# First stage: tiles of octets two to four turned on VectorE and by transfers, instead of on TensorE

## The chip, the cores and the metric

The kernel runs on one core of a Trainium2 chip. The metric is the device time of one execution in microseconds (us), the median of several runs. The core has TensorE (PE in the rows), VectorE (DVE), ScalarE (ACT), GpSimd (POOL) and SyncE (SP), and 16 DMA engines that SyncE and GpSimd issue transfers to.

## The reference

A gated cross-attention layer and a gated mixture-of-experts layer, over x of 32 batches x 64 tokens x 512 and a context of the same shape:

```python
x = x + tanh(g_xattn) * attn(layernorm(x), ctx)
x = x + tanh(g_ffn) * moe(layernorm(x))
# in attn: keys and values from context and latents together
hidden_states = jnp.concatenate([context, latents], axis=1)
q = (latents @ Wq)                       # 32 heads of 128
k = (hidden_states @ Wk)                 # 4 heads of 128
v = (hidden_states @ Wv)
```

The change concerns only the first stage, which makes k and v and the turned, normalised x from which the second stage makes q. Attention, the output projection (second stage) and the experts (third stage) are as they were.

## The kernel before, in words

x and the context are 2048 tokens each. They are worked in four **octets** of 512 tokens (o = 0 to 3; "octet 1" in the text and in the comments below is o = 0, so octets 2 to 4 are the changed ones). An octet has 8 **units**: four 128-token tiles of the context (src 0) and four of the normalised x (src 1). For every unit four 128x128 transposes on TensorE (L414, `transposes`) put the tile, features on partitions, into a PSUM tile `ps_t`; ScalarE copies it rounded into `tok_hi` (L273, `tok`), VectorE writes the remainder into `tok_lo` (L342, `tok_low`). All products are made in three passes of rounded parts (L84 to L86). A **V job** (`v_job`, one per unit, 12 matmuls) makes the values of 128 tokens in `ps_v`, which ScalarE copies out (L282, `v_copy`); a **K job** (`k_job`, 8 per octet, 12 matmuls) makes a head's keys of 512 tokens of one source in `ps_k`, which VectorE copies out (L352, `k_copy`). `ps_v` and `ps_k` have two banks each, so job n waits for the copy of job n - 2. `tok_hi` and `tok_lo` have two buffers, one per octet in turn.

The order on every engine is written out by hand, and every engine works strictly in its own order. TensorE: for an octet its 8 V jobs, each with the next unit's transposes ahead of it, then its 8 K jobs, with the next octet's first transposes before the sixth. VectorE: the low parts and normalisations (L336, `normalise`, into one of two `normed` buffers) between, and in octet 1's K phase the statistics of the last eight x tiles (L316, L319). ScalarE: the high part of the next unit, then the V copy. SyncE issues all loads and stores: the next octet's context tiles (L206, L207) before the last V store, the stores of V (L213), of the turned x (L219) and of K (L237). GpSimd makes constants and loads the two gates (L252), and has nothing more to do in this stage. In the profile the block transpose on VectorE stands only in the second stage (L1013, issued on by L774, read back by L783), and GpSimd's indirect transfers only in the third (L1693, L1703).

Of the kernel before, what the change touches and what calls it, by code (L numbers as in the profile page):

```python
# [27 lines left out]
P = 128  # L28
# [4 lines left out]
C = D // P  # L33
# [59 lines left out]
def stage_one(nc, a, common, scratch):  # L93
# [25 lines left out]
    with ExitStack() as stack:  # L119
# [12 lines left out]
        normed = [b.sb(f"normed{i}", [P, D]) for i in range(2)]  # L132
        stats = b.sb("stats", [P, TILES, 6])
# [10 lines left out]
        x_in = [b.sem(f"x_in{i}") for i in range(OCTETS)]  # L144
        ctx_in = [b.sem(f"ctx_in{i}") for i in range(2)]
        kv_in = [b.sem(f"kv_in{i}") for i in range(4)]
        gates_in = b.sem("gates_in")
# [19 lines left out]
        x_stored = [b.sem(f"x_stored{i}") for i in range(2)]  # L167

# [4 lines left out]
        UNITS = 8  # L173

        def unit(o, u):

            return (u // 4, u % 4) if o == 0 else (u % 2, u // 2)
# [7 lines left out]
        def _(sp):  # L185
# [13 lines left out]

            for o in range(OCTETS):  # L200
                for u in range(UNITS):
                    src, i = unit(o, u)

                    if u == 7 and o + 1 < OCTETS:
                        sp.wait_ge(transposed, UNITS * o + 7)
                        sp.dma_start(ctx_raw[:, 0], ctx_v[o + 1][:, 0]).then_inc(ctx_in[0], 16)  # L206
                        sp.dma_start(ctx_raw[:, 1:4], ctx_v[o + 1][:, 1:4]).then_inc(ctx_in[1], 16)  # L207
# [8 lines left out]
                    if u in (5 if o == 0 else 4, 7):  # L216
# [11 lines left out]
                if o == OCTETS - 1:  # L228
# [24 lines left out]

        @block.scalar
        def _(act):
# [5 lines left out]
            def split_hi(piece, hi):  # L261
                act.wait_ge(kv_in[piece], 16)
# [3 lines left out]
            def tok(o, u):  # L266
                src, i = unit(o, u)

                act.wait_ge(transposed, UNITS * o + u + 1)
                if u == 0 and o >= 2:  # L270

                    act.wait_ge(x_stored[o % 2], 64)
                act.activation(tok_hi[o % 2][:, src, :, i * P:(i + 1) * P], ps_t[u % 2][:],  # L273
                               ACT.Copy).then_inc(tok_hi_made, 1)
# [10 lines left out]
            tok(0, 0)  # L285
            split_hi(0, wv_hi)
            split_hi(1, wv_hi)
            for o in range(OCTETS):
                for u in range(UNITS):
                    if u + 1 < UNITS:  # L290
                        tok(o, u + 1)
# [1940 lines left out]
```

## Time and profile before

| | |
|---|---|
| median of 3 runs | 1464.78 us (1463.96 to 1466.05) |
| the profiled execution: span | 1485.9 us |
| its own time beside the span | not recorded apart; the span stands for it |
| first stage, to the last K job | 200.8 us of the span |
| mean granted TensorE clock | 0.987 |

The rows are those of one profiled execution; their times are microseconds from its start. "Idle before" in brackets is how long the engine had stood still and what ended it. In the rows an instruction's duration runs to its end; the next one of the same engine often starts a little before that, so that the pitch from start to start is what a queue of them takes.

### The profile page before, as it was taken

What the parts mean: (1) busy time and instruction counts of PE and PEld (TensorE: products, weight loads), DVE (VectorE), ACT (ScalarE), POOL (GpSimd) and SP (SyncE); (2) the same over time, 40 slices, a digit from 0 to 9 for tenths busy, and PEclk for the clock granted to TensorE, in tenths of its full rate; (3) what the DMA queues carried; (4) which work ended last, traced back from release to release, by engine and by line L of the source; (5) the groups of instructions that cost most, each with busy time, mean ns of one, the idle gap of its engine ahead of it and who ended that gap; (6) DMA issues with size and microseconds to landing.
All of it is one profiled execution on the core that took longest, in us unless ns stands there. A gap on an engine that the chain in (4) does not pass through costs nothing.

```text
span 1485.9 us, 24374 instructions
## 1 busy us (share of the span) xinstructions
PE 1416.6 (95%) x8624; PEld 1253.0 (84%) x8624; DVE 1041.1 (70%) x1682; ACT 785.9 (53%) x2029; POOL 191.1 (13%) x200
## 2 busy tenths in 40 slices
PE   7999988999999999999999999999998899989885
PEld 6888887999999899999899999899997588888774
DVE  4422238777788777787877787887787587656657
ACT  4212226555566555566655566655555445767660
POOL 0000000000000000000000000000026124777740
PEclk9999999999999999999999999999999999999998
DMA  8576555344454433463443365444324206876419
GB/s 264 156 231 170 142 198 157 123 135 125 149 179 146 139 121 121 161 180 127 142 150 118 123 179 167 133 136 138 119 90 144 99 1 211 258 252 212 150 29 339
DMA packets 189622, 230.98 MB, mean 155 GB/s; under 512 B 22675, under 2 KB 123063, under 8 KB 185418
## 3 DMA queue, kind: packets, MB, share of 16 engines
q1 hardware_dynamic: 179530, 212.77, 45.3%
q0 software_dynamic: 9984, 16.82, 3.5%
q8 instruction: 62, 1.02, 0.3%
q14 instruction: 46, 0.38, 0.1%
HBM read 161.85 MB, written 83.36 MB: 165 GB/s over the span
## 4 chain that ended last, share of the span: by engine, by line
PE 67%; DVE 6%; ACT 5%; issue 3%; DMA 2%; another core or an unknown queue 2%; SPq 0%; ACTq 0%; POOL 0%; DVEq 0%; POOLq 0%
PE ps_q L84 8%; PE ps_y L84 8%; PE ps_y L86 7%; PE ps_y L85 7%; PE ps_q L85 7%; PE ps_q L86 7%; PE ps_s L1082 5%; PE bank L84 3%; PE bank L86 3%; PE bank L85 2%; PE ps_s L1084 2%; PE ps_o L84 2%; PE ps_o L86 2%; PE ps_o L85 2%
## 5 line engine op out<-in xcount | busy, mean ns | idle before, releaser
L84 PE MATMUL ps_q<-xt,wq_hi 128*128 128x256 f32 x1024 | 296.3, 289 | 2.3 <-PEq L119 1.7
L85 PE MATMUL ps_q<-xt,wq_lo 128*128 128x256 f32 x1024 | 289.4, 283 | 0.0
L86 PE MATMUL ps_q<-xt,wq_hi 128*128 128x256 f32 x1024 | 289.4, 283 | 0.0
L903 ACT ACTIVATE s_sb<-s_sb,nmax 128x128 f32<-128x128 f32 x512 | 200.5, 394 | 148.5 <-DVE nmax L991 148.5
L84 PE MATMUL ps_y<-wo_hi,o_hi 128*128 128x512 f32 x512 | 204.6, 400 | 7.2 <-DVE wo_lo L935 3.6
L86 PE MATMUL ps_y<-wo_lo,o_hi 128*128 128x512 f32 x512 | 203.5, 398 | 0.0
L85 PE MATMUL ps_y<-wo_hi,o_lo 128*128 128x512 f32 x512 | 202.6, 396 | 0.0
L84 PEld LDWEIGHTS ps_q<-xt,wq_hi 128*128 128x128 f32 x1024 | 195.2, 191 | 2.9 <-issue 2.1
L85 PEld LDWEIGHTS ps_q<-xt,wq_lo 128*128 128x128 f32 x1024 | 195.8, 191 | 0.0
L86 PEld LDWEIGHTS ps_q<-xt,wq_hi 128*128 128x128 f32 x1024 | 195.6, 191 | 0.0
L883 ACT ACTIVATE o_hi<-ps_o 128x512 fp32r<-128x512 f32 x128 | 76.1, 595 | 183.2 <-PE ps_o L86 183.0
L980 DVE TENSOR_TENSOR o_lo<-ps_o,o_hi 128x512 fp32r<-128x512 f32 x128 | 88.2, 689 | 79.4 <-ACT o_hi L883 79.4
L940 DVE TENSOR_TENSOR q_lo<-ps_q,q_hi 128x512 fp32r<-128x512 f32 x128 | 88.5, 691 | 69.5 <-ACT q_hi L859 69.5
L1082 PE MATMUL ps_s<-kt,q_hi 128*128 128x256 f32 x512 | 125.5, 322 | 3.1 <-DVE q_lo L940 2.1
L84 PEld LDWEIGHTS ps_y<-wo_hi,o_hi 128*128 128x128 f32 x512 | 97.2, 190 | 27.0 <-DVE wo_lo L935 4.2
L556 POOL TENSOR_TENSOR trial<-root 128x9 f32<-128x9 f32 (+1 forms) x6 | 1.7, 284 | 904.3 <-DVE root L578 904.0
L86 PEld LDWEIGHTS ps_y<-wo_lo,o_hi 128*128 128x128 f32 x512 | 97.0, 189 | 23.2
L1084 PE MATMUL ps_s<-kt,q_lo 128*128 128x128 f32 x512 | 114.3, 223 | 0.0
L85 PEld LDWEIGHTS ps_y<-wo_hi,o_lo 128*128 128x128 f32 x512 | 97.3, 190 | 18.4
L1082 PEld LDWEIGHTS ps_s<-kt,q_hi 128*128 128x128 f32 x512 | 96.6, 189 | 10.0 <-issue 2.7
L1084 PEld LDWEIGHTS ps_s<-kt,q_lo 128*128 128x128 f32 x512 | 97.8, 191 | 6.2
L989 DVE TENSOR_TENSOR s_sb<-ps_s,s_cross 128x512 f32<-128x512 f32 x128 | 88.1, 688 | 18.0 <-ACT s_cross L889 17.8
(261 smaller groups left out, 3160.2 us busy)
## 6 DMA issues: line engine op xcount, KB each, us to landing
xt<-x_scratch SPq DMA_DIRECT2D x32, 1024.0 KB, 5.6
p_table<-p_blocks SPq DMA_DIRECT2D x128, 256.0 KB, 2.0
p_lo<-p_table SPq DMA_DIRECT2D x512, 64.0 KB, 2.1
w_raw<-in_L_ffn_ew SPq DMA_DIRECT2D x93, 256.0 KB
v_full<-v_out SPq DMA_DIRECT2D x64, 128.0 KB, 2.6
k_full<-k_out SPq DMA_DIRECT2D x16, 512.0 KB, 2.8
w_raw<-in_L_xattn_Wq SPq DMA_DIRECT2D x16, 512.0 KB, 5.9
kt_raw<-k_full SPq DMA_DIRECT2D x32, 256.0 KB, 2.8
```

What stands on the lines that cost most here:

```text
L84: pe.matmul(out, w_hi, x_hi, start=first, stop=False)
L85: pe.matmul(out, w_lo, x_hi, start=False, stop=False)
L86: return pe.matmul(out, w_hi, x_lo, start=False, stop=last)
L556: then(pool.tensor_tensor(w, r, r, ALU.mult))
L883: act.activation(o_hi[s.last_parity][:, :, s.last_token], ps_o[:], ACT.Copy).then_inc(o_hi_made, 1)
L903: last = act.activation(s_sb[:, i], s_sb[:, i], ACT.Exp, bias=nmax[:, i:i + 1], accum_out=sums[:, i:i + 1])
L940: dve.tensor_tensor(by_heads(q_lo[quad_parity], p), ps_q[p % 2][:].rearrange("p (h b t) -> p h b t", h=2, b=QB), f32(by_heads(q_hi[quad_pa ...
L980: dve.tensor_tensor(o_lo[s.last_parity][:, :, s.last_token], ps_o[:], f32(o_hi[s.last_parity][:, :, s.last_token]), ALU.subtract).then_inc ...
L989: dve.tensor_tensor(s_sb[:], ps_s[:, :, 0], s_cross[:], ALU.add).then_inc(folded, 1)
L1082: pe.matmul(ps_s[:, i], q_hi[quad_parity][:, batch, heads].rearrange("p h t -> p (h t)"), k[:, :, batch], start=True, stop=False)
L1084: last = pe.matmul(ps_s[:, i, 0], q_lo[quad_parity][:, batch, heads].rearrange("p h t -> p (h t)"), k[:, 0, batch], start=False, stop=True)
```

## The change

Octet 1 stays as it was, with transposes on TensorE. For octets 2 to 4 TensorE has no transposes. VectorE turns each tile of 128x512 in 32x32 blocks into `blocks` (`turn`), context tiles from `ctx_raw`, x tiles from `normed`. When the four tiles of one source are turned, GpSimd issues 16 transfers (`move`) that carry block row i, block column j of all of them to partitions 32j to 32j + 31 of `turned`. ScalarE makes `tok_hi` from `turned` (`tok_turned`) and VectorE `tok_lo` (`tok_turned_low`). There is one `blocks` and one `turned`, both of 8 KB a partition. So the turns of x wait until the context's move has landed, and a move waits until the low parts of what stood in `turned` are made. The context of an octet is loaded by four transfers instead of two, in an order of rows that suits the blocks, and earlier. Units of all octets now go context first, then x. The statistics of tiles 8 to 15 move from octet 1's K phase to the start of octet 2's V phase, and their square root on ScalarE behind octet 2's third V copy. x stores come after units 6 and 8. Some semaphores are shared (the last two x loads, the two Wk loads).

```diff
+        blocks = b.sb("blocks", [P, 4, C, 4, 32])
+        turned = b.sb("turned", [P, C, 4, 4, 32])
...
+        ctx_rows = a["ctx_4096"].rearrange("b s d -> (b s) d").rearrange("(o i t s) d -> o t i s d", i=4, t=4, s=32)
+        def unit(u):
+            return u // 4, u % 4
+        def blocks_by(o, src):
+            return UNITS * (o - 1) + 4 * src + 4
+        def moves_by(o, src):
+            return 256 * (2 * (o - 1) + src + 1)
...
+            def load_ctx(o):
+                for t in range(4):
+                    sp.dma_start(ctx_raw[:, t], ctx_rows[o, t]).then_inc(ctx_in[1], 16)
...
+                    if o == 0 and u == 4:
+                        sp.wait_ge(transposed, 4)
+                        load_ctx(1)
+                    if 0 < o < OCTETS - 1 and u == 2:
+                        if o + 2 < OCTETS:
+                            sp.wait_ge(blocks_made, blocks_by(o + 1, 0))
+                            load_ctx(o + 2)
...
+                if o == 0:
+                    sp.wait_ge(blocks_made, blocks_by(1, 0))
+                    load_ctx(2)
...
+            def move(o, src):
+                pool.wait_ge(blocks_made, blocks_by(o, src))
+                if src or o > 1:
+                    pool.wait_ge(tok_lo_made, UNITS * o + 4 * src)
+                for i in range(4):
+                    for j in range(4):
+                        pool.dma_start(turned[32 * j:32 * j + 32, :, i].rearrange("p c t s -> p c (t s)"),
+                                     blocks[32 * i:32 * i + 32, j].rearrange("p c t s -> p c (t s)")
+                                     ).then_inc(moved, 16)
...
+            def tok_turned(o, u):
+                src, i = unit(u)
                 if u == 0 and o >= 2:
 
                     act.wait_ge(x_stored[o % 2], 64)
+                act.wait_ge(moved, moves_by(o, src))
+                act.activation(tok_part(tok_hi[o % 2], u), turned_part(u), ACT.Copy).then_inc(tok_hi_made, 1)
...
+                    if o == 1 and u == 2:
+                        std_of(8, TILES)
+                    if 0 < o < OCTETS - 1 and u in (3, 4):
+                        tok_turned(o + 1, 2 * u - 6)
+                        tok_turned(o + 1, 2 * u - 5)
                 if o == 0:
                     std_of(4, 8)
+                    for u in range(4):
+                        tok_turned(1, u)
                 if o + 1 < OCTETS:
-                    tok(o + 1, 0)
+                    for u in range(4, UNITS):
+                        tok_turned(o + 1, u)
...
+            def turn(o, u):
+                src, t = unit(u)
+                if t == 0 and (src or o > 1):
+                    dve.wait_ge(moved, moves_by(o, src) - 256)
+                if src:
+                    dve.wait_ge(normed_made, 4 * o + t + 1)
+                else:
+                    dve.wait_ge(ctx_in[1], 16 + 64 * o)
+                tile = normed[t % 2][:] if src else ctx_raw[:, t, :]
+                dve.transpose(blocks[:, :, :, t, :], tile.rearrange("p (c j r) -> p j c r", c=C, j=4)
+                              ).then_inc(blocks_made, 1)
...
+            turn_ctx(1)
+            for job in range(UNITS):
+                k_copy(0, job)
+                if job == 1:
+                    turn_x(1)
+                if job in (2, 3):
+                    tok_turned_low(1, 2 * job - 4)
+                    tok_turned_low(1, 2 * job - 3)
+                if job in (6, 7):
+                    tok_turned_low(1, 2 * job - 8)
+                    tok_turned_low(1, 2 * job - 7)
+            for o in range(1, OCTETS):
+                if o + 1 < OCTETS:
+                    turn_ctx(o + 1)
+                    if o == 1:
+                        dve.wait_ge(late_in, 32)
+                        stats_of(8, TILES)
+                        rstd_of(8, TILES, 3)
+                    turn_x(o + 1)
+                    for u in range(4):
+                        tok_turned_low(o + 1, u)
                 for job in range(UNITS):
                     k_copy(o, job)
+                    if o + 1 < OCTETS and job < 4:
+                        tok_turned_low(o + 1, 4 + job)
```

On VectorE, from the reciprocal of octet 1's second normalisation through the K copies of octet 1, the order before was:

```order
L323 RECIPROCAL rstd<-std 128x4
L352 COPY k_out<-ps_k 128x8x64
L336 TENSOR_SCALAR normed<-y,mean_var,rstd 128x512
L352 COPY k_out<-ps_k 128x8x64
L336 TENSOR_SCALAR normed<-y,mean_var,rstd 128x512
L352 COPY k_out<-ps_k 128x8x64
L316 BN_STATS stats<-y 128x6 x2
L319 BN_AGGR mean_var<-stats 128x2 x2
L352 COPY k_out<-ps_k 128x8x64
```

and is now:

```order
L378 RECIPROCAL rstd<-std 128x4
L411 STREAM_TRANSPOSE blocks<-ctx_raw 128x16x32 x4
L425 COPY k_out<-ps_k 128x8x64 x2
L392 TENSOR_SCALAR normed<-y,mean_var,rstd 128x512 x2
L411 STREAM_TRANSPOSE blocks<-normed 128x16x32
L392 TENSOR_SCALAR normed<-y,mean_var,rstd 128x512
L411 STREAM_TRANSPOSE blocks<-normed 128x16x32
L392 TENSOR_SCALAR normed<-y,mean_var,rstd 128x512
L411 STREAM_TRANSPOSE blocks<-normed 128x16x32 x2
L425 COPY k_out<-ps_k 128x8x64
L416 TENSOR_TENSOR tok_lo<-turned,tok_hi 128x4x128 x2
L425 COPY k_out<-ps_k 128x8x64
```

The third K copy now stands behind the first turn of a normalised tile, which waits for the move of the context tiles.

On ScalarE, from the end of octet 1's V phase into octet 2's, the order is now (`turned` is the tile that the moves fill, `std` the square root for the normalisation):

```order
L302 ACTIVATE std<-mean_var,eps 128x4
L322 ACTIVATE tok_hi<-turned 128x4x128 x8
L359 ACTIVATE ones_r<-ones 128x128
L361 ACT_TABLE_LOAD
L361 ACTIVATE gain_attn<-gates 128x1
L362 ACTIVATE gain_ffn<-gates 128x1
L330 ACTIVATE v_out<-ps_v 128x512 x3
L302 ACT_TABLE_LOAD
L302 ACTIVATE std<-mean_var,eps 128x8
L330 ACTIVATE v_out<-ps_v 128x512
L322 ACTIVATE tok_hi<-turned 128x4x128 x2
L330 ACTIVATE v_out<-ps_v 128x512
```

All eight high parts of octet 2 stand ahead of its first V copy, and the next octet's between the fourth, fifth and later ones; before, each high part stood just ahead of the V copy of the unit before it.

## Rows read from the trace of the kernel before

**Rows 1.** The page: busy us, share of the span, instructions
```profile
PE 1416.6 (95%) x8624; PEld 1253.0 (84%) x8624; DVE 1041.1 (70%) x1682; ACT 785.9 (53%) x2029; POOL 191.1 (13%) x200
```

**Rows 2.** By stretch: length, busy us of PE, PEld, DVE, ACT, POOL, clock, DMA share
```profile
36.60:58.90 22.30, 22.30 (x102) 18.41 (x101) 12.25 (x28) 3.46 (x8) 0.00 (x0) 1.00 0.63 206
...
84.20:106.30 22.10, 22.10 (x101) 18.21 (x101) 6.44 (x10) 1.20 (x2) 0.00 (x0) 1.00 0.87 280
...
179.00:200.80 21.80, 21.77 (x97) 17.68 (x95) 4.84 (x7) 0.60 (x1) 0.00 (x0) 1.00 0.43 138
```

**Rows 3.** Timeline of ScalarE, V copies: start, us, what, idle before
```profile
24.16 0.60 ACT L282 ACTIVATE v_out<-ps_v 128x512 f32<-128x512 f32 x1 [2.17 <-PE ps_v L86]
...
62.26 0.60 ACT L282 ACTIVATE v_out<-ps_v 128x512 f32<-128x512 f32 x1 [2.17 <-PE ps_v L86]
...
65.47 0.60 ACT L282 ACTIVATE v_out<-ps_v 128x512 f32<-128x512 f32 x1 [2.12 <-PE ps_v L86]
```

**Rows 4.** Timeline of VectorE, first stage
```profile
37.62 0.18 DVE L323 RECIPROCAL rstd<-std 128x4 f32<-128x4 f32 x1 [1.54 <-ACT std L259]
...
89.66 0.69 DVE L352 COPY k_out<-ps_k 128x512 f32<-128x512 f32 x1 [1.57 <-PE ps_k L86]
90.27 0.54 DVE L336 TENSOR_SCALAR normed<-y,mean_var,rstd 128x512 f32<-128x512 f32 x1
92.38 0.69 DVE L352 COPY k_out<-ps_k 128x512 f32<-128x512 f32 x1 [1.57 <-PE ps_k L86]
```

**Rows 5.** Timeline of VectorE, a block transpose of the second stage and its successor
```profile
222.94 0.71 DVE L1013 STREAM_TRANSPOSE p_blocks<-s_sb 128x512 f32<-128x512 f32 x1
223.57 1.18 DVE L935 TENSOR_TENSOR wo_lo<-w_raw,wo_hi 128x1024 fp32r<-128x1024 f32 x1
```

**Rows 6.** Timeline of GpSimd: its plain gate loads, and indirect ones of stage three
```profile
1.96 0.73 POOL L252 DMA_DIRECT2D gates<-in_g_xattn  x1 [0.25 <-issue]
2.69 0.58 POOL L252 DMA_DIRECT2D gates<-in_g_ffn  x1
...
1263.44 1.03 POOL L1703 DMA_INDIRECT slots_y<-y_out,slot_row  x1 [3.16 <-ACT y_out L1811]
1264.78 1.00 POOL L1703 DMA_INDIRECT slots_y<-y_out,slot_row  x1 [0.31 <-issue]
1266.09 1.46 POOL L1693 DMA_INDIRECT rows_in<-xn_table,slot_token  x1 [0.30 <-issue]
```

**Rows 7.** DMA issues: tile, queue, count, KB each, median us to landing
```profile
p_lo<-p_table SPq DMA_DIRECT2D x512, 64.0 KB, 2.1
...
gates<-in_g_xattn POOLq DMA_DIRECT2D x1, 0.5 KB, 6.6
```

**Rows 8.** The line of SyncE's 32-partition transfers: issue ns min/median/max
```profile
L783 SPq DMA_DIRECT2D p_lo<-p_table x512: 302/432/1939, 225.7 to 1159.3; - x171
```

**Rows 9.** Timeline of ScalarE ahead of octet 2
```profile
55.95 0.29 ACT L304 ACTIVATE ones_r<-ones 128x128 fp32r<-128x128 f32 x1
56.26 1.28 ACT L306 ACT_TABLE_LOAD   x1
...
57.66 0.19 ACT L307 ACTIVATE gain_ffn<-gates 128x1 f32<-128x1 f32 x1
```

**Rows 10.** Groups by line, first 209 us: busy us, mean ns, idle before
```profile
L316 DVE BATCH_NORM_STATS2 stats<-y 128x6 f32<-128x512 f32 x16 | 10.3, 679 | 0.0
...
L319 DVE BATCH_NORM_AGGREGATE mean_var<-stats 128x2 f32<-128x6 f32 x16 | 2.3, 170 | 0.1
```

**Rows 11.** Timeline of TensorE: the first and the seventh matmul after its first idle
```profile
7.92 0.77 PE L84 MATMUL ps_v<-wv_hi,tok_hi 128*128 128x512 f32 x1 [3.00 <-DVE wv_lo L328]
...
10.62 0.46 PE L84 MATMUL ps_v<-wv_hi,tok_hi 128*128 128x512 f32 x1
```

**Rows 12.** DMA of the first 209 us: total, and context loads as in rows 7
```profile
DMA packets 38065, 39.36 MB, mean 188 GB/s; under 512 B 1949, under 2 KB 28573, under 8 KB 37906
...
ctx_raw<-in_ctx SPq DMA_DIRECT2D x4, 768.0 KB, 6.4
```

More of the change, by code:

```diff
@@ L142, in stage_one @@
         ps_k = [b.ps(f"ps_k{i}", [P, 512]) for i in range(2)]
-        x_in = [b.sem(f"x_in{i}") for i in range(OCTETS)]
+        gates_in = b.sem("gates_in")
+        late_in = b.sem("late_x_in")
+        x_in = [b.sem(f"x_in{i}") for i in range(2)] + [late_in] * (OCTETS - 2)
         ctx_in = [b.sem(f"ctx_in{i}") for i in range(2)]
-        kv_in = [b.sem(f"kv_in{i}") for i in range(4)]
-        gates_in = b.sem("gates_in")
+        kv_in = [b.sem(f"wv_in{i}") for i in range(2)] + [b.sem("wk_in")] * 2
         consts_made = b.sem("consts_made")
@@ L167, in stage_one @@
         x_stored = [b.sem(f"x_stored{i}") for i in range(2)]
+        blocks_made = b.sem("blocks_made")
+        moved = b.sem("moved")
         x_v = a["x"].rearrange("b s d -> (b s) d").rearrange("(o i p) d -> o p i d", i=4, p=P)
@@ L252, in _ @@
                 pool.dma_start(gates[:, i:i + 1], src).then_inc(gates_in, 16)
+            def move(o, src):
[8 more added lines that the diff above has]
+            for o in range(1, OCTETS):
+                move(o, 0)
+                move(o, 1)
         @block.scalar
@@ L289, in _ @@
                 for u in range(UNITS):
-                    if u + 1 < UNITS:
-                        tok(o, u + 1)
+                    if o == 0 and u + 1 < UNITS:
+                        tok(u + 1)
                     if o == 0 and u == 2:
@@ L353, in k_copy, with turn_ctx, turn_x @@
                                 ps_k[job % 2][:].rearrange("p (q b t) -> p q b t", q=2, b=QB)).then_inc(k_copied, 1)
-            tok_low(0, 0)
+            def turn_ctx(o):
+                for u in range(4):
+                    turn(o, u)
+            def turn_x(o):
+                normalise(4 * o)
+                normalise(4 * o + 1)
+                for t in range(4):
+                    turn(o, 4 + t)
+                    if t < 2:
+                        normalise(4 * o + 2 + t)
+            tok_low(0)
@@ new lines, in _ @@
+            rstd_of(4, 8, 2)
+            turn_ctx(1)
[9 more added lines that the diff above has]
+                    tok_turned_low(1, 2 * job - 7)
+            for o in range(1, OCTETS):
+                if o + 1 < OCTETS:
[5 more added lines that the diff above has]
+                    turn_x(o + 1)
+                    for u in range(4):
+                        tok_turned_low(o + 1, u)
@@ L417, in v_job @@
             def v_job(o, u):
-                src, i = unit(o, u)
+                src, i = unit(u)
                 n = UNITS * o + u
@@ L442, in k_job @@
                 last.then_inc(k_done, 1)
-            transposes(0, 0)
+            transposes(0)
             for o in range(OCTETS):
                 for u in range(UNITS):
-                    if u + 1 < UNITS and not (o == 0 and u == 0):
-                        transposes(o, u + 1)
+                    if o == 0 and 0 < u < UNITS - 1:
+                        transposes(u + 1)
                     v_job(o, u)
                     if o == 0 and u == 0:
-                        transposes(0, 1)
+                        transposes(1)
                 if o == 0:
@@ L454, in _ @@
                 for job in range(UNITS):
-                    if o + 1 < OCTETS and job == 5:
-                        transposes(o + 1, 0)
                     k_job(o, job)
```

114 lines of the change are left out of this document (52 added, 62 removed).

## The prediction

> **What bounds the kernel now.** I read the page first, then the busy time by stretch, then the timelines of the first stage. The page gives TensorE 95% of the span [rows 1]. The change touches the first stage alone, so the question is what sets the pace there. The table by stretch answers it: from 36.6 us, where the K jobs of octet 1 begin, TensorE is busy without a break, at a granted clock of 1.00 (the upper of its two levels, 2.4 GHz), until the stage's last K job is done at 200.8 us; of seven stretches three are shown, and only the last lacks 0.03 us [rows 2]. Every microsecond of TensorE work taken out there is a microsecond won, as long as its operands still come in time. In the rows of VectorE and ScalarE both wait for TensorE: VectorE copied a K result every 2.72 us and stood idle 1.57 us before each copy [rows 4].
>
> **What is removed.** A job of twelve 128x512 matmuls takes 2.72 us alone: K copies start at 89.66 and 92.38 [rows 4]. A V job has the same twelve and one tile's four transposes, and takes 3.21 us: V copies start at 62.26 and 65.47 [rows 3]. A tile's transposes so cost 0.49 us of TensorE. Octets 2 to 4 have 24 tiles: 24 x 0.49 = **11.8 us** less TensorE work. The copies out of PSUM (tok_hi on ScalarE, tok_lo on VectorE) stay in number and only read `turned` instead.
>
> **What is added, and its unit price.** VectorE gets 24 block transposes. The same form and size stands in the second stage at 0.71 us, and the next instruction starts 0.63 us after it [rows 5]. I take 0.63 us a tile; a copy takes 0.61 by the same measure (89.66 to 90.27), and a normalisation, 0.54 long, 0.45 [rows 4].
>
> GpSimd gets 96 transfers in six moves of 16, each with 32 partitions of 4 runs of 512 bytes, 64 KB. No row shows a plain transfer of this size issued by GpSimd. The nearest are its two plain gate loads, 128 pieces each as these have, at 728 and 577 ns back to back [rows 6]. I take the second, since the first also bears the start: 0.58 us. Bounds: below, SyncE issues 32-partition transfers of 64 KB in 0.30 us at least and 0.43 in the median [rows 8]; above, GpSimd's indirect ones start 1.3 us apart [rows 6]. From issue to landing SyncE's 64 KB transfers take 2.1 us in the median [rows 7]; a gate load of GpSimd took 6.6 us amid the first loads [rows 7]. I take 2.1, for its size and its place after the first loads, and keep 6.6 as the end. A **move** so takes 16 x 0.58 + 2.1 = **11.4 us**.
>
> **Where that lies.** `blocks` and `turned` exist once. So VectorE may not turn the normalised tiles before the move of the context tiles has landed, GpSimd may not start the second move before those turns and four tok_lo are done, and in VectorE's and ScalarE's queues copies that TensorE needs stand behind these waits. I walk through it, with TensorE free-running at 2.72 us a job from 36.6 us.
> (a) VectorE finishes the reciprocal at 37.8 [rows 4], turns four context tiles (2.5) by 40.3; move 1 lands at 51.7. Behind the wait VectorE has four turns and two normalisations (3.4) and then the third K copy (0.7): 55.8. TensorE's fifth K job needs that copy and could have started at 36.6 + 4 x 2.72 = 47.5. **Idle 8.3.**
> (b) After the turns (55.1) come two copies and four tok_lo (6 x 0.61): move 2 starts at 58.8, lands at 70.2. ScalarE stands before it; then four tok_hi (0.5 each), the constant, table load and tanh (1.8, [rows 9]) and the first V copy (0.6): 74.6. TensorE did its K jobs by 66.7, two V jobs by 72.1, and needs that copy for the third. **Idle 2.5.**
> (c) VectorE, after tok_hi, has four tok_lo and a K copy (3.0), four turns (2.5): 76.4. Then eight statistics with aggregates, 0.77 each by their starts (0.68 and 0.17 long, [rows 10]) = 6.2; ScalarE waits for them with table load and root (1.5) and the fourth V copy (0.6): 84.7, against TensorE at 74.6 + 3 x 2.72 = 82.8. **Idle 2.0.**
> (d) Move 3 runs from 76.4 to 87.8; ScalarE takes two tok_hi, then the V copy: 89.4, against 87.4. **Idle 2.0.**
> (e) Turns to 91.2, four tok_lo to 93.7, move 4 lands at 105.1; tok_hi, tok_lo and the second K copy: 107.0. TensorE's fourth K job could start at 89.4 + 5 x 2.72 = 103.0. **Idle 4.0.**
> (f) In octet 3 the V copy after move 5 comes just in time (136.8 against 136.9), the K copy behind move 6 does not: 154.6 against 150.5. **Idle 4.0.**
> Octet 4 has no moves. Sum 22.8 of new idle, less 11.8 = **+11.0 us**; each 0.1 us on a move adds some 0.6.
>
> **The rest.** After its first idle TensorE took 2.7 us for six V matmuls, from 7.92 to 10.62 [rows 11], where six at a twelfth of 2.72 take 1.4: 1.3 us lost. I add it once, for the 8.3 us gap; the bounds are 0 and 1.3 for each of (a), (e) and (f). SyncE's context loads become four per octet. The first four go out after octet 1's fourth V copy (24.8, [rows 3]) and its two stores; with 6.4 us to landing [rows 12] they are in by about 35, and the turns start at 37.8: no cost. If that cover went, (a) would start later by the lateness. SyncE gets waits on the turns of the next octet, behind which V stores stand; each is over before the V copy that comes next. The second stage's first transfers wait for stores of octet 4, unchanged. 6 MB more between SBUF and SBUF stand beside 39 MB [rows 12] in a stage whose DMA share is 0.43 to 0.87 [rows 2]; that lies inside 2.1 to 6.6. So 11.0 + 1.3 = **+12.3 us** on the profiled 1485.9, which itself lies 21 us over the median of the runs; I carry the difference to the median: 1464.8 + 12.3 = **1477.1**.
>
> **Rivals.**
> (These times leave the 1.3 out.) *Issues are cheap (the other side).* If GpSimd issued almost as SyncE does at its best (0.30), say 0.34 us, a move is 7.5 us. Then idle is 4.5 in (a), 0.6 in (c) and none elsewhere: 5.1 - 11.8 = -6.7, **1458.1**. It decides at a move of 9.5 us, an issue of 0.46. For it: 32 partitions are fewer than 128. Against: both plain rows are above 0.46. The Trainium skill, "DMA: Bandwidth & Descriptors", section on the anatomy of one DMA on the GpSimd path, calls descriptor generation small and gives about 2.0 us plus bytes over 436 GB/s, which for 1 MB is an estimated 4.4 us a move and some 10 us gained; no plain transfer of size in this trace tests it.
> *Issues are dear.* At the indirect pitch of 1.3 a move is 22.9 us; idle by the same walk is 19.9, 14.0, 2.0, 13.5, 15.6, 11.4 (octet 3 then misses the V copy too) and 15.6: 92.0 - 11.8 = +80, **1545**; at 0.9 it is +42, 1507; at 0.58 but 6.6 to landing, +38, 1503. For it: 4 runs a partition. Against: indirect ones also read indices.
> *VectorE holds GpSimd off.* Most of VectorE's work during the moves reads PSUM, but in (d) the eight statistics run beside move 3. If they kept GpSimd from issuing, move 3 would land 6.2 us later and nothing absorbs it: +18, **1483**. In the trace GpSimd's indirect issues vary only from 1.00 to 1.46 us in a stretch where VectorE works too [rows 6], which speaks for little of it. The Trainium skill, "SBUF — State Buffer", warns that VectorE instructions which take two SBUF ports lock GpSimd's descriptor writing out and puts one DMA at 620 ns alone and about 3100 ns beside such a copy; at that price the change would be far slower, and no row here shows it.
> That the change doesn't do what it says is excluded: TensorE's program lists no transposes after octet 1.
>
> **How the numbers follow.** Forecast (issue 0.50 to 0.75, GpSimd not held off): 0.38, own range 1468 to 1492. Held off: 0.05. Dear: 0.22. Cheap enough to win (under 0.45): 0.27. Near the balance, within 0.2% (2.9 us, what a measurement of this kernel can tell from no change): 0.08. Faster 0.27, same 0.08, slower 0.65. The range goes from 1456 to 1506: it leaves out the upper half of the dear case (0.11) and moves shorter than about 6.5 us (0.05).
>
> **What would show it.** Right: new groups of 96 GpSimd transfers of some 0.58 us, first 16 spanning 9 us from about 40; TensorE idle some 8 us before its fifth K job, waiting for a K copy, and the stage's end near 212 us instead of 200.8. Wrong: GpSimd transfers under 0.45 us and a stage end under 200. The table by stretch says which.

## The result and the profile after

The changed kernel takes **1505.2 us** (median of 4 runs, 1500.4 to 1508.5) beside 1464.7 for the kernel before on the same chip. The ratio is 1.0269, with a 95% interval of 1.0241 to 1.0296, so it is 40.5 us slower. The prediction was 1477.1 us: the sign is right, the loss is more than three times the 12.3 us forecast. Its own range for the forecast (1468 to 1492) missed; the outer range (1456 to 1506) held the time only just.

The busy times of the page after, beside [rows 1]:

```profile
PE 1410.7 (94%) x8528; PEld 1246.9 (83%) x8528; DVE 1053.1 (70%) x1706; ACT 788.3 (52%) x2031; POOL 244.1 (16%) x296
```

TensorE has 96 instructions less (24 tiles of four transposes), GpSimd 96 more, VectorE 24 more. The rest is in where the stage ends. The first matmul of stage two, before and then after, on TensorE's timeline (start, length, idle before it):

```profile
202.51 0.36 PE L84 MATMUL ps_q<-xt,wq_hi 128*128 128x256 f32 x1 [1.74 <-PEq L119]
```
```profile
241.94 0.36 PE L84 MATMUL ps_q<-xt,wq_hi 128*128 128x256 f32 x1 [1.72 <-PEq L119]
```

That is 39.4 us later, nearly all of the 40.5: the loss lies in stage one. (The spans, 1505.9 and 1485.9, are not to be set side by side: behind this start the profiled execution of the kernel before took 1283 us, that of the changed kernel 1264, and those of the thirteen profiled runs below, with the same later stages, 1257 to 1268.) The first stage by stretch, with the columns of [rows 2] (length, busy us of PE, PEld, DVE, ACT, POOL, clock, DMA share, GB/s):

```profile
39.60:61.90 22.30, 11.35 (x49) 8.74 (x47) 4.87 (x9) 0.78 (x2) 8.67 (x16) 0.88 0.83 230
61.90:83.50 21.60, 17.23 (x68) 14.11 (x69) 11.82 (x20) 5.38 (x10) 8.65 (x16) 0.81 0.46 129
83.50:110.00 26.50, 19.54 (x76) 15.33 (x75) 15.60 (x34) 8.18 (x16) 11.05 (x21) 0.87 0.72 184
...
131.00:153.00 22.00, 22.00 (x98) 18.21 (x97) 6.05 (x10) 2.39 (x4) 8.81 (x16) 1.00 0.52 143
153.00:190.00 37.00, 28.63 (x106) 22.61 (x105) 11.78 (x19) 7.49 (x13) 8.64 (x16) 0.82 0.59 152
```

Before, TensorE was busy in every microsecond of such a table and its clock stood at 1.00. Now it stands still for up to half of a stretch, and the granted clock falls in the same stretches. The waits of TensorE from 36 to 242 us say for whom (waited for: us in total, times, longest):

```profile
PE ps_k L84 <- DVE k_out L425: 26.6, 4, 13.2
PE ps_v L84 <- ACT v_out L330: 9.2, 3, 6.7
```

These are copies of K and V results, which stand in VectorE's and ScalarE's queues behind waits for the moves. The moves on GpSimd's timeline (start, length of 16 issues, idle before):

```profile
46.96 8.67 POOL L289 DMA_DIRECT2D turned<-blocks  x16 [43.67 <-DVE blocks L411]
69.81 8.65 POOL L289 DMA_DIRECT2D turned<-blocks  x16 [14.17 <-DVE tok_lo L416]
86.76 8.64 POOL L289 DMA_DIRECT2D turned<-blocks  x16 [8.30 <-DVE blocks L411]
107.59 8.65 POOL L289 DMA_DIRECT2D turned<-blocks  x16 [12.19 <-DVE tok_lo L416]
143.23 8.81 POOL L289 DMA_DIRECT2D turned<-blocks  x16 [26.98 <-DVE blocks L411]
163.24 8.64 POOL L289 DMA_DIRECT2D turned<-blocks  x16 [11.20 <-DVE tok_lo L416]
```

The first instruction that a move releases gives its landing. Two of the six, on VectorE's and ScalarE's timelines:

```profile
61.93 0.71 DVE L411 STREAM_TRANSPOSE blocks<-normed 128x512 f32<-128x512 f32 x1 [13.06 <-DMA turned<-blocks]
```
```profile
177.96 2.19 ACT L322 ACTIVATE tok_hi<-turned 128x512 fp32r<-128x512 f32 x4 [11.61 <-DMA turned<-blocks]
```

The other four land at 80.30, 100.92, 122.06 and 156.56. From first issue to last landing the six take 15.0, 10.5, 14.2, 14.5, 13.3 and 14.7 us, 13.7 in the mean; the forecast had 11.4. I call the part behind the last issue the tail: 6.3, 1.8, 5.5, 5.8, 4.5 and 6.1 us, 5.0 in the mean, where 2.1 was taken.

### The profile page after: what moved, and what is told of

Its sections match the earlier page's. It is cut to its first block, busy times and chain, and to the rows that moved or that the text cites. A ratio compares the mean times of both kernels' runs of the same rounds, so it can differ in the third digit from the quotient of the medians.

```text
span 1505.9 us, 24296 instructions
## 1 busy us (share of the span) xinstructions
PE 1410.7 (94%) x8528; PEld 1246.9 (83%) x8528; DVE 1053.1 (70%) x1706; ACT 788.3 (52%) x2031; POOL 244.1 (16%) x296
## 4 chain that ended last, share of the span: by engine, by line
PE 63%; DVE 7%; issue 4%; DMA 4%; ACT 3%; POOL 3%; ACTq 0%; POOLq 0%; SPq 0%; DVEq 0%
PE ps_q L84 8%; PE ps_y L84 7%; PE ps_y L86 7%; PE ps_y L85 7%; PE ps_q L86 7%; PE ps_q L85 7%; PE ps_s L1173 5%; PE ps_s L1175 2%; PE ps_o L84 2%; PE ps_o L86 2%; PE ps_o L85 2%; PE bank L84 2%; DMA slots_y<-y_out,slot_row 2%; POOL rows_in L1784 2%; DMA w_raw<-in_L_xattn_Wo 2%
## 5 line engine op out<-in xcount | busy, mean ns | idle before, releaser
L84 PEld LDWEIGHTS ps_q<-xt,wq_hi 128*128 128x128 f32 x1024 | 194.8, 190 | 4.1 <-issue 2.1
```

The source lines that it names most:

```text
L84: pe.matmul(out, w_hi, x_hi, start=first, stop=False)
```

## Experiments

Each time stands beside the kernel before in the same set of runs (1463.9, 1465.7, 1465.2, 1464.6 and 1464.5 us in the five sets). Theory A: what costs is the length of the moves, as waits at a few places, with a lower clock behind each stop. Against it stand, in turn, the moves' own bytes, a price of the transfers beyond the waits, and other causes of slow matmuls.

**The changed kernel again.**

> The changed kernel once more, for a second profile of the same program. Theory A (the moves' landing is late because the 16 DMA engines also carry SyncE's loads and stores): issue again 0.54 us each, moves of 10.5 to 15 us with the shortest where the fewest other transfers run, stage one ends at 241 +- 4 us. Theory B (octet 1's 3.0 us and the late context load were chance of one execution): this profile has its first K job near 36.6 us and context tiles turned from 41 us; otherwise near 39.6 and 44 us again.

1504.25 us. Moves of 15.0, 10.6, 13.7, 15.0, 12.3 and 14.7 us; TensorE's stops 2.2, 13.2, 0.2, 6.2, 5.4, 1.2 and 7.7 us. The pattern is the kernel's, not one run's. Octet one again ended late (first K job at 39.5, turns from 44.1), which Theory B of the expectation would not have; the other runs below take it up again.

**No moves at all.** Constant data in `turned`; VectorE's turns stay.

```
-            for o in range(1, OCTETS):
-                move(o, 0)
-                move(o, 1)
+            pool.memset(turned[:]..., 0.5).then_inc(moved, 1)
...
-                act.wait_ge(moved, moves_by(o, src))
+                act.wait_ge(moved, 1)
```

> Leaves out the 96 transfers and the waits for them; turned is filled once with a constant, so keys, values and x of octets 2 to 4 are wrong. Everything else of the change stays (turns on VectorE, copies out of turned, context loads in four, the new orders). Theory A (only the moves cost): the 11.8 us of transposes are won, less up to 3 for octet 1: ratio 0.992 to 0.994 (1453 to 1456 us), stage one ends at 189 to 192 us. Rival R (VectorE's added turns or the new orders on ScalarE cost by themselves): ratio at or over 0.997, and TensorE waits for a copy by VectorE or ScalarE somewhere.

1457.8 us, ratio 0.9960 (0.9946 to 0.9974): 6 us under the kernel before, and between the two expectations (at most 0.994, at least 0.997). Stage two starts at 194.8, 7.7 us earlier than before. The whole loss of the change therefore needs the moves. Of the 4.1 us missing to the 11.8 of removed transposes, 1.3 are a later start of the K jobs (37.9 against 36.6) and 2.2 are one stop, whose cause VectorE's timeline shows:

```profile
42.54 2.49 DVE L407 STREAM_TRANSPOSE blocks<-ctx_raw 128x512 f32<-128x512 f32 x4 [3.44 <-DMA ctx_raw<-in_ctx]
```

Even without moves VectorE waits 3.4 us for octet two's context, which the prediction had in the tile by 35 us; TensorE stops 2.2 us behind it. The row also gives the price of a turn: 2.49 us for four, 0.62 each (taken: 0.63).

**Less store traffic.** V and x stores carry a quarter of their bytes; the rest is written at the stage's end, and that filling is in the time.

```
-   sp.dma_start(dst.rearrange("g t d -> t g d"),
-                v_out[u % 4][64 * bb:64 * bb + 64])
+   sp.dma_start(dst.rearrange("g t d -> t g d")[:, 0:1],
+                v_out[u % 4][64 * bb:64 * bb + 64, 0:1])
```

> The stores of V and of the turned x carry a quarter of their bytes during the stage; the rest of those tensors is filled with other data by extra stores at the stage's end (and two before the first load of x), so results are wrong and the total has that fill in it; only the moves' times in stage one are to be read. Theory A (shared DMA engines): the landing after the last issue of moves 3 to 6, which was 5.5, 5.8, 4.5 and 6.1 us, falls to 2 to 3.5 us. Rival P (32-partition transfers are slow among themselves, or GpSimd's queue lands late by itself): it stays at 4.5 to 6 us.

1537.7 us in all, with the filling, so only the moves are read. Their tails are 5.1, 2.0, 6.2, 6.9, 2.8 and 1.4 us. In moves five and six, beside which mainly the stores run, they fell from 4.5 and 6.1 to 2.8 and 1.4. Moves one, three and four run beside context loads, K stores or the loads for stage two, which were left, and their tails did not fall. The issues took 0.54 us as ever. The expectation had moves three and four fall too; they rose, by 0.6 and 1.1 us. Beside move four this run is no clean test: two of the stores that fill up x, 384 KB each, go out at 109.7 and 110.7, in the middle of it. So moves five and six show that the tail follows the traffic beside the move; for the others this run leaves it open, and the total says nothing here.

**A quarter of the moves' own bytes**, with the same 96 issues.

```
-  pool.dma_start(turned[32*j:32*j+32, :, i]..., blocks[32*i:32*i+32, j]...)
+  pool.dma_start(turned[32*j:32*j+32, 0:1, i]..., blocks[32*i:32*i+32, j, 0:1]...)
```

> The changed kernel, but each of GpSimd's 96 transfers moves one quarter of its columns (32 x 512 bytes instead of 32 x 2048); the rest of turned holds a constant written once, so that the product is not the reference's. The issues stay sixteen a move. Theory A (what a transfer waits for is the other traffic on the shared DMA engines): a move keeps most of its tail beside other traffic, the last transfer landing 3 to 5 us after the last issue in moves 1, 3 and 4, and the time is within 12 us of the changed kernel's 1505. Theory B (the transfers' own bytes make the tail): the tails fall to about 2 us everywhere, moves take 10.7 us, and the time falls by some 20 us to 1485.

1488.0 us in one run, 17 below the changed kernel, between the two expectations (over 1493, and 1485). The tails are 4.3, 1.4, 4.4, 4.7, 1.4 and 3.6 us, 3.3 in the mean instead of 5.0: a quarter of the bytes takes a third of the tail away, and what stays is again long in moves one, three and four. An issue took 496 instead of 548 ns. So both the traffic beside a move and its own bytes count; the time fell with the length of a move, 11.1 us instead of 13.7. What fewer issues, in place of smaller ones, would give was not measured.

**Waits of a set length, without a transfer.** Six, or eight, fills of the same tile on GpSimd take the place of each move.

```
-                        pool.dma_start(turned[32 * j:32 * j + 32, :, i]...
+                for i in range(6):
+                    if done + i:
+                        pool.wait_ge(moved, done + i)
+                    pool.memset(turned[:]..., 0.5).then_inc(moved, 1)
```

> The changed kernel with every move replaced by six fills of the same tile on GpSimd, one behind the other (one took 1.82 us, so some 11 us, the length of a move that the prediction took), with the same waits before and after and no transfer; the product is not the reference's. It shows what moves of the predicted length cost when nothing else about them is left. If the walk of the prediction is right in its terms, 1476 us. Theory A (the excess came from the length of the moves beside other traffic, from a clock that falls after each stop of TensorE, and from late context loads): the clock and the late loads are still there, so 1482 to 1492 us, with matmuls 0.43 us apart behind each stop over 2.3 us. If the time is 1500 or more, the length of the moves is not what matters.

> As the run with six fills, with eight of them (some 14.6 us, about the mean length of the moves as measured). Theory A: 1500 to 1508 us, the changed kernel's time without a single transfer of its own, so that a microsecond on each move costs 5 to 7 us in all. Rival (the transfers cost beyond the wait, by taking DMA time from the loads and stores): under 1495 us.

Six fills: 1486.9 us (ratio 1.0147, 1.0122 to 1.0171). Eight: 1514.7 (1.0332, 1.0315 to 1.0350), above the range that I gave, since the fills took longer than I reckoned. Two of the "moves" of each on GpSimd's timeline, six fills first:

```profile
43.83 11.45 POOL L291 MEMSET turned<- 128x2048 f32 x6 [40.55 <-DVE blocks L411]
62.71 11.16 POOL L291 MEMSET turned<- 128x2048 f32 x6 [7.43 <-DVE tok_lo L416]
```
```profile
44.48 15.18 POOL L291 MEMSET turned<- 128x2048 f32 x8 [41.20 <-DVE blocks L411]
67.08 14.90 POOL L291 MEMSET turned<- 128x2048 f32 x8 [7.43 <-DVE tok_lo L416]
```

The means over six are 11.3 and 15.05 us. So 3.74 us on each move cost 27.8 us, 7.4 us for each (6 to 9 by the intervals of the two ratios). On the line through these two points the changed kernel's 13.7 us give 1504.6; it takes 1505.2 with all its transfers. The run with a quarter of the bytes, at 11.1 us, should take 1485.7 and takes 1488.0. **The time follows from the length of the moves**; in this order of the work no price of the transfers beyond the wait can be seen. The agreement is closer than these runs can tell: the four of one kernel lie 3 to 8 us apart, the changed kernel began its K jobs 2.8 and 2.3 us later than the two runs with fills, and eight fills had stops of 39.9 us in all beside its 35.9. A price of a few us would not show. At the 11.4 us of the forecast the line gives 1487.5, not 1477.1. So of the 28 us missed some 17 are length, and some 10.5 would have been missed at the right length too.

**Context loaded earlier.**

```
-                    if o == 0 and u == 4:
+                    if o == 0 and u == 3:
                         sp.wait_ge(transposed, 4)
                         load_ctx(1)
```

> The changed kernel with one step moved: the loads of the second octet's context stand ahead of the fourth V store in SyncE's queue, not ahead of the fifth; nothing else. The prediction had these loads in by 35 us at no cost. Theory A (VectorE's turns, the moves behind them and the first stop of TensorE wait for these loads, 3.4 us of it): the first move starts some 3 us earlier, at about 43.5, and the time falls by 2 to 6 us. If the loads cost nothing, the time stays within 1 us of 1505.

1501.4 us, 3.8 less, ratio 1.0254 (1.0232 to 1.0276). That is the size expected, but the interval overlaps the changed kernel's, so a gain is likely and not shown. In its profile VectorE no longer waits for the context (0.04 us instead of 3.4), TensorE's early stop of 2.1 us is gone, and the first move starts at 41.9 instead of 47.0, of which 2.2 us come from an octet one that was done earlier in that run. The stop before octet two's fourth K job was longer in return, 7.2 us instead of 5.2.

**Matmuls that nobody reads, in the stops.**

```
+                    if u == 6:
+                        keep_busy(o, (0, 28, 8, 0)[o])
                     v_job(o, u)
...
+                    if job == (4 if o == 0 else 3):
+                        keep_busy(o, (56, 22, 24, 0)[o])
                     k_job(o, job)
```

> The changed kernel with matmuls that nobody reads (into a bank that is free by then) put where TensorE stops: 56 ahead of the fifth K job of the first octet, 28 and 8 ahead of the seventh V jobs of octets two and three, 22 and 24 ahead of their fourth K jobs. At 0.23 us each they are a little shorter than the stops as measured (13.2, 6.7, 2.3, 5.2, 6.1 us). Theory A (after each stop the clock stays at half for some 4 us, about 11 us in all): the matmuls behind the places of the stops stand 0.23 us apart, the granted clock is 0.99 or more from 60 to 200 us, and the time falls by 6 to 11 us, to 1494 to 1499. Rival (the slow matmuls have another cause, the SBUF or the transfers): they stay 0.43 apart and the time stays, or rises by what the added matmuls take.

TensorE's timeline behind the long stop, first in the changed kernel, then with the filling:

```profile
66.27 0.79 PE L84 MATMUL ps_k<-tok_hi,wk_hi 128*128 128x512 f32 x1 [13.23 <-DVE k_out L425]
66.86 0.63 PE L85 MATMUL ps_k<-tok_hi,wk_lo 128*128 128x512 f32 x1
67.29 0.63 PE L86 MATMUL ps_k<-tok_lo,wk_hi 128*128 128x512 f32 x1
...
70.16 0.40 PE L84 MATMUL ps_k<-tok_hi,wk_hi 128*128 128x512 f32 x1
70.39 0.40 PE L85 MATMUL ps_k<-tok_hi,wk_lo 128*128 128x512 f32 x1
```
```profile
64.23 0.39 PE L84 MATMUL ps_k<-tok_hi,wk_hi 128*128 128x512 f32 x1
64.45 0.39 PE L85 MATMUL ps_k<-tok_hi,wk_lo 128*128 128x512 f32 x1
64.68 0.39 PE L86 MATMUL ps_k<-tok_lo,wk_hi 128*128 128x512 f32 x1
```

With TensorE kept busy the matmuls stand 0.23 us apart at once; idle before them, they stood 0.43 apart for 3.9 us. The granted clock over the two stretches (the column behind POOL's, in shares of 2.4 GHz) is 0.50, which is 1.2 GHz, and 1.00:

```profile
66.30:70.00 3.70, 3.70 (x9) 2.92 (x10) 2.92 (x5) 0.00 (x0) 0.20 (x1) 0.50 0.46 171
```
```profile
64.20:68.00 3.80, 3.80 (x18) 3.15 (x17) 3.13 (x6) 0.00 (x0) 0.78 (x2) 1.00 0.52 194
```

So it is the clock, and the rival falls. Over the stage I count 50 matmuls about 0.43 apart after the change, 10.5 us more than at 0.23, and 15 with the filling, 3.0 us. But the time is 1501.6 us, 3.6 less where I expected 6 to 11, and not surely less (1.0249, 1.0227 to 1.0270, which overlaps the changed kernel's). TensorE still waits 8.7 us beside the filling:

```profile
PE ps_k L84 <- DVE k_out L425: 7.0, 3, 3.1
PE ps_v L84 <- ACT v_out L330: 1.7, 2, 1.2
```

At these places the chain of moves sets the pace. A faster TensorE only comes earlier to the next wait. So the 7.5 us of slow matmuls that went gave back some 3.6; by the two intervals it can be anything from nothing to all of it. That they are worth less than their length is likely, from the waits that remain, and not shown.

**Another order of the work.** In octets two to four TensorE runs the four V and the four K jobs of the context, then those of x; the other engines wait for a move only where its tiles are next. The first context load stands one V store earlier, as in the run above.

```
+                    if o and u == 3:
+                        for job in range(4):
+                            k_job(o, job)
...
-                g, src = job // 2, job % 2
+                g, src = (job % 4, job // 4) if o else (job // 2, job % 2)
```

> The changed kernel in another order: in octets two to four TensorE runs the four V jobs of the context, the four K jobs of the context, the four V jobs of x, the four K jobs of x; ACT and VectorE wait for a move only where its tiles are next, and the first context load is issued one V store earlier. The moves and their transfers are the same. Theory A (the cost is the wait at a few places, not the transfers themselves): each move now has some 20 us of cover, the stops of TensorE shrink to under 4 us in sum, and the time is 1457 to 1466 us. Rival (GpSimd's transfers slow the whole stage, by VectorE or by the DMA engines): 1480 us or more.

1474.3 us (1.0065, 1.0047 to 1.0083): 31 less than the changed kernel with the same 96 transfers, so the rival, at 1480 or more, is out. It also missed my 1457 to 1466. The largest stop left, 5.1 us, has a new cause, on VectorE:

```profile
129.27 0.69 DVE L423 COPY k_out<-ps_k 128x512 f32<-128x512 f32 x1 [15.12 <-DMA k_full<-k_out]
130.88 0.69 DVE L423 COPY k_out<-ps_k 128x512 f32<-128x512 f32 x1 [0.92 <-DMA k_full<-k_out]
```

A K result can't be copied before the K store of the octet before has left its tile; in this order that copy comes sooner, and the store went out late.

**The same with that mended**: K stores ahead of the loads for stage two, low parts of x ahead of the fourth K copy.

```
                 if o == 1:
+                    store_k(1)
                     sp.wait_ge(kv_lo_made, 4)
...
+                    if o and job == 3:
+                        tok_turned_low(o, 4)
+                        tok_turned_low(o, 5)
```

> The run with the split order (1474 us), with the two causes of its remaining stops moved: the K stores of the second octet go out ahead of the loads for stage two (the first K copy of the third octet waited 5.1 us for such a store), and VectorE takes the low parts of the first x tiles ahead of the fourth K copy (stops of 2.8, 1.4 and 1.4 us). All 96 transfers are still there. Theory A: TensorE then stops less than 1.5 us at a time, the clock doesn't fall, stage one ends some 7 us before that of the kernel before, and the time is 1456 to 1460 us. If the transfers had a price of their own, it stays above 1464.

1464.5 us, ratio 0.9994 (0.9981 to 1.0008): even with the kernel before, where I had expected 1456 to 1460, and just over the 1464 that I had set for "a price of their own". One stop of 3.2 us stayed. The move of octet three's x took 18.0 us beside K stores and loads, its transfers landing 7.1 us after issue in the median:

```profile
turned<-blocks POOLq DMA_DIRECT2D x16, 64.0 KB, 7.1
```

**The x moves earlier; then the same without transfers.**

```
+                    if o + 1 < OCTETS and job == 6:
+                        for t in range(4):
+                            turn(o + 1, 4 + t)
...
+                            tok_turned_low(o + 1, t)
                     k_copy(o, job)
```

> The second split order (1464.5 us, one stop of 3.2 us left ahead of the x tiles of octet three, whose move took 18 us beside K stores and the loads for stage two), with two steps moved: the load of x for stage two (1 MB) goes out at the end of octet three, and VectorE turns the x tiles and takes the context's low parts ahead of the last two K copies, so that the x moves start 1 to 2 us earlier. Theory A: the stop falls under 2 us, the clock stays up, stage one ends near 192 to 195 us and the time is 1458 to 1462 us, under the kernel before. If what remains is a price of the transfers themselves, it stays at 1464.

> The third split order with the 96 transfers and all waits for them left out; turned holds a constant, so the product is not the reference's. Theory A (off the path, the transfers cost little): 1456 to 1459 us, within 3 us of the run with the transfers. If the transfers have a price of their own, the difference is 4 us or more.

With transfers 1463.2 us (0.9986, 0.9973 to 1.0000), above the expected 1458 to 1462 and at the edge of what can be told from the kernel before; without, 1454.7 (0.9942, 0.9920 to 0.9965), where stage two starts at

```profile
191.23 0.36 PE L84 MATMUL ps_q<-xt,wq_hi 128*128 128x256 f32 x1 [1.72 <-PEq L119]
```

This is 11.3 us ahead of the kernel before, and the time is 9.8 us less: the 11.8 us of removed transposes were priced about right. The two runs are 8.5 us apart, more than the 4 that I had set for "a price of their own". The DMA issues of both from 108 to 127 us, with transfers first (count, KB, median us to landing):

```profile
k_full<-k_out SPq DMA_DIRECT2D x4, 512.0 KB, 13.2
turned<-blocks POOLq DMA_DIRECT2D x16, 64.0 KB, 7.2
w_raw<-in_L_xattn_Wq SPq DMA_DIRECT2D x2, 512.0 KB, 12.1
```
```profile
k_full<-k_out SPq DMA_DIRECT2D x2, 512.0 KB, 7.2
w_raw<-in_L_xattn_Wq SPq DMA_DIRECT2D x2, 512.0 KB, 7.6
```

K stores and weight loads take 13 and 12 us to land beside a move, 7 to 8 without, and TensorE stops twice, 2.0 and 2.1 us, before K copies that wait for such stores. The neighbours are not quite the same: without the waits the four K stores are issued from 104.9, not from 110.8, and the first two, ahead of the window, land in 5.2 and 5.3 us. Stage two starts 8.0 us later with the transfers. Stops of 4.5 us in all, slow matmuls of some 2 us behind the second of the two, and K jobs that began 0.7 us later make up 7 of them. So here too the price is paid in waits.

**SyncE's queue order**, the question that was open after these. The context load of octet four goes behind octet two's K stores, the Wq load for stage two into octet three.

```
-                            sp.wait_ge(blocks_made, blocks_by(o + 1, 0))
-                            load_ctx(o + 2)
...
                 if o == 1:
                     store_k(1)
+                    sp.wait_ge(blocks_made, blocks_by(2, 0))
+                    load_ctx(3)
```

> The third split order with two loads moved in SyncE's queue: the context load of octet four goes out behind the K stores of octet two, not ahead of its fifth V store (SyncE then spent 20 us on the stores behind it, and the K stores were issued from 110.8 to 119.9, over 10 us after the first two K results had been copied), and the Wq load for stage two goes out in octet three. The 96 transfers are as before. Theory A (the 8.5 us between the runs with and without transfers come from K stores that land too late for VectorE's next K copies, a matter of the queue's order): the K stores are issued from about 104, the two stops of 2.0 us go, no matmul stands 0.43 us apart, stage one ends near 192 to 194, and the time is 1456 to 1460 us, clearly under the kernel before. Theory C (the bytes of the moves slow the stores beside them, wherever they stand): the stops stay, and the time stays at 1461 to 1465.

1462.8 us (0.9986, 0.9973 to 0.9999). The two stops before K copies went, with K stores issued from 102.9 (the four landed in 5.4, 5.3, 3.8 and 5.0 us), but others came, 4.9 us in all:

```profile
PE ps_v L84 <- DVE tok_lo L419: 4.0, 3, 2.5
PE ps_v L84 <- ACT v_out L335: 0.9, 1, 0.9
```

The longest is ahead of octet four's first V job: its context now comes late, its turns start at 132.7 and its move lands at 151.1. The time stayed, as Theory C has it; the stops did not stay where they were, as Theory A has it. Put in one place or another, some transfer is late. How the remaining 8 us divide between bytes and order stays open.

## Why the prediction was right and wrong

**Right in its mechanism and sign.** TensorE waits for copies queued behind waits for the moves, at the places named: fifth K job of octet one, V and K jobs in octets two and three. The transposes were worth 11.3 us by the start of stage two, 9.8 by the time (said: 11.8). The turn cost 0.62 (0.63), the GpSimd issue 0.54 (0.58). What was wrong are three sizes: the landing, the clock behind a stop, and the first context load.

**The term that failed first: the landing.** "I take 2.1", and the sentence that 6 MB more "lies inside 2.1 to 6.6". It does lie inside, but near the upper end: the tails are 5.0 us in the mean. The 2.1 came from stage two's loads of `p_lo` [rows 7], while the moves run where the DMA share was already up to 0.87 [rows 2]. It was also a median, and a move ends with the last of its sixteen. The 96 transfers of the changed kernel (ns of an issue, min/median/max; us from issue to landing):

```profile
L289 POOL DMA_DIRECT2D turned<-blocks x96: 548/548/711, 47.0 to 171.3; - x96
DMA to landing us min/median/max: 2.0/3.6/6.8
```

and the last of each move 5.5 us in the mean. The move so took 13.7 us instead of 11.4 (2.9 more of tail, 0.6 less of issues), at a measured 7.4 us of time for each us of move (said: 0.6 for 0.1, so 6): 17 us. The dear rival's last figure, 1503 for 6.6 us to landing, was the nearest of all, and it had only part of a chance of 0.22. Its nearness is luck: it stands for moves of 15.9 us, 2.2 more than they took, and lacks the clock.

**The walk, step by step**, as predicted, with six fills (11.3 us a move, the test of the walk), and in the changed kernel:

| stop of TensorE, us | predicted | six fills | changed kernel |
|---|---|---|---|
| early in octet one's K jobs | 0 | 2.0 | 2.1 |
| (a) fifth K job | 8.3 | 7.9 | 13.2 |
| (b) third V job | 2.5 | 0.9 | 0.3 |
| (c), (d) seventh V job | 2.0 + 2.0 | 3.8 | 6.7 |
| (e) fourth K job | 4.0 | 2.1 | 5.2 |
| (f) octet three, V and K | 0 + 4.0 | 0.2 + 3.7 | 2.3 + 6.1 |
| sum | 22.8 | 20.5 | 35.9 |

At the length it assumed, the walk was right within 2.3 us in sum. Part of that is luck: the early stop of 2.0 us, which it did not have, makes up for (b) and (e), which were 1.6 and 1.9 us too long. (c) and (d) are one stop, since only the later wait shows. In the changed kernel (b) was less, probably because TensorE came to it later: it had stood 5 us longer in (a).

**The clock was taken once, 1.3 us.** The range in the text was 0 to 1.3 for each of three stops. Behind each of the five stops of 2.3 to 13.2 us in the changed kernel the matmuls stood 0.43 us apart for 3.6 to 6 us, at a cost of some 2.1 us each, not 1.3: 10.5 in all, and 7.2 with six fills. That is 5.9 more than taken, and at that length of move the largest part of the 10.5 us that the forecast missed. [Rows 11] show the end of such a stretch only, and I read it as the whole.

**Context loads "in by about 35 ... no cost".** They were issued from 29.1, and VectorE waited 3.4 us for them, until 44.2: 15.1 us from the first issue to the turns, where 6.4 was taken. With six fills they were issued from 26.3, about where the forecast had them, and VectorE waited until 41.3, 15.0 us again. So the landing was wrong here too, more than the place in the queue. That was the cover which the text said could go. Its price is the stop of 2.1 us and a first move later by 3.4. Octet one was also done 3.0 us late (39.6 against 36.6), in both profiles of the changed kernel. Their traces show where: TensorE stood still at 12.0 and 11.8 for a low part of Wv, 1.5 and 1.2 us, and in the first the clock rose only at 15.4 instead of 10.7. The run with the stops filled is the same program up to there, has no such stop, and begins its K jobs at 36.8. So it is scatter and no part of the change that I can show.

**The sum.** From stops 35.9, slow matmuls 10.5, start 3.0, less 11.8: 37.6 of the 39.4 us by which stage two starts later. Some 2 us are not placed.

**The rivals.** Cheap issues: an issue is 0.54, over the 0.46 at which it decides. The Trainium skill, "DMA: Bandwidth & Descriptors", in its section on the anatomy of one DMA, makes the generation of descriptors a small part; by that a move was an estimated 4.4 us. The trace doesn't agree: the 16 issues alone take 8.7 of a move's 13.7 us. VectorE holding GpSimd off: of 96 issues the longest took 711 ns, the median 548, beside turns, copies, statistics and subtractions alike, and the move with the eight statistics (86.8) issued in 8.64 us as the others. The Trainium skill, "SBUF — State Buffer", section "A bandwidth-pool intuition that's wrong (but worth ruling out)", puts a GpSimd DMA of 620 ns near 3100 ns beside a VectorE copy. No issue here shows such a delay, also not beside the two f32 normalisations that run during move one's issues.

## What to carry to other kernels

Price a transfer by a row from the stretch where it will run, or add the traffic beside it: 64 KB took 2.1 us to land in one stage and 3.6, at worst 6.8, in another. When a change puts a wait into a queue, count the copies behind it first. Here the same 96 transfers cost 40 us in one order of the work and nothing in another, while the best order still gained only 1 or 2 (by its interval, 0 to 4) of the 11.3 us that the transposes had taken. Take the landing of the last transfer of a group, not the median of all. And a change that only takes out work of the bound engine should be run once with the new work left out: that gives the most it can gain.

## What was not expected of the hardware

- **A clock that falls, and may not be worth its face value.** Behind each of five stops of 2.3 to 13.2 us TensorE ran at 1.2 GHz for 3.6 to 6 us; behind the one of 2.1 us in octet one it stayed at 2.4. The length of the stop alone does not say it: behind that same stop, at 1.95 us with six fills, 2.1 with a quarter of the bytes and 2.0 with the stops filled, the clock fell. With six fills, the stop, and a stretch soon behind it with its granted clock of 0.51:

```profile
44.40 0.50 PE L84 MATMUL ps_k<-tok_hi,wk_hi 128*128 128x512 f32 x1 [1.95 <-DVE k_out L425]
```
```profile
45.60:49.00 3.40, 3.40 (x9) 2.65 (x9) 2.34 (x2) 0.00 (x0) 3.28 (x3) 0.51 0.81 273
```

- **Landing under load.** `k_full` stores of 512 KB landed in 2.8 us with nothing beside them (129.7 to 140.6 in the changed kernel), in 7.2 us beside loads and V stores, and in 13.2 with a move beside them too; in the last run two that were issued as a move began, just ahead of context loads, took 3.8 and 5.0. A quarter of the bytes of a move shortened its tail by a third only.
- **GpSimd's issue is steady**: 548 ns for 32 partitions with four runs of 512 bytes, 496 with one run, and never over 711 ns, whatever VectorE did. That is close to the second gate load's 577 ns [rows 6], so for the issue the nearest row was a good guide; for the landing it was not.
